# Self attention of a transformer's last stage: values as the weights, turned probabilities as the moving side, four heads side by side, the result copied out and turned back

## The reference, cut to what matters

```python
def _attention(src, Wq, bq, Wk, bk, Wv, bv, Wo, bo):      # 16 heads of 8 dims, 100 tokens
    q = (src @ Wq + bq).reshape(B, T, NHEAD, HEAD_DIM)
    k = (src @ Wk + bk).reshape(B, T, NHEAD, HEAD_DIM)
    v = (src @ Wv + bv).reshape(B, T, NHEAD, HEAD_DIM)
    scores = jnp.einsum('bqhd,bkhd->bhqk', q, k) * HEAD_DIM ** (-0.5)
    probs = jax.nn.softmax(scores, axis=-1)
    out = jnp.einsum('bhqk,bkhd->bqhd', probs, v).reshape(B, T, d)
    return out @ Wo + bo
```

## Time and profile before

| | us |
|---|---|
| median of three runs | 2578.37 (2575.73 to 2595.78) |
| the profiled execution, its time | 2595.61 |
| its span | 2593.8 |
| the self attention's 64 pieces in it | 1896.5 to 2348.6, 452.1 |
| the experts behind it | 2348.6 to 2593.8, 245.2 |

### The profile page before, as it was taken

The page is one execution under the profiler, slowest core; times in us unless marked ns, Lnnn a source line. Parts: engine busy times, 40 slices in busy tenths (PEclk is TensorE's granted clock), DMA queues, the critical chain, the costliest instruction groups (busy, mean ns, idle before and its releaser), DMA issues. The chain is left out here.

```text
span 2593.8 us, 44760 instructions
## 1 busy us (share of the span) xinstructions
PE 2236.1 (86%) x17786; PEld 1541.0 (59%) x17786; DVE 1608.6 (62%) x3886; ACT 1306.4 (50%) x2135; POOL 521.8 (20%) x428
## 2 busy tenths in 40 slices
PE   4689995565699999999999999999789999999997
PEld 3446663343355556555555556565557877777776
DVE  5734443777578787877878778888233444443433
ACT  3545553555156666666666666666523333333333
POOL 1400002332322122221222212222021111111111
PEclk8789995555599999999999999999865555558999
DMA  4036660000232223322333223332210010000000
GB/s 148 1 107 188 187 183 0 6 18 20 76 106 82 93 95 110 103 96 72 105 110 107 84 82 108 107 107 88 74 34 17 17 32 1 1 1 1 10 8 10
DMA packets 89100, 181.15 MB, mean 70 GB/s; under 512 B 5906, under 2 KB 63162, under 8 KB 88510
## 3 DMA queue, kind: packets, MB, share of 16 engines
q1 hardware_dynamic: 88894, 178.30, 20.9%
HBM read 95.24 MB, written 11.65 MB: 41 GB/s over the span
## 5 line engine op out<-in xcount | busy, mean ns | idle before, releaser
L1414 DVE TENSOR_REDUCE b_part_max<-psum 128x1 f32<-128x482 f32 (+3 forms) x1248 | 737.5, 650 | 187.2 <-PE psum L1291 173.3
L1204 ACT ACTIVATE b_PT<-psum 128x800 f32<-128x800 f32 x768 | 616.5, 836 | 386.6 <-PE psum L1310 380.4
L1291 PE MATMUL psum<-b_KH,b_QBD 64*128 64x482 f32 (+1 forms) x1152 | 421.5, 442 | 46.3 <-DVE b_part_max L1414 43.4
L1310 PE MATMUL psum<-b_QS,b_KS 64*128 64x200 f32 x3072 | 438.5, 288 | 0.5 <-ACT b_PT L1204 0.3
L1310 PEld LDWEIGHTS psum<-b_QS,b_KS 64*128 64x128 f32 x3072 | 339.6, 187 | 16.2 <-issue 12.1
L1326 PE MATMUL psum<-b_PT,b_V 128*32 128x200 f32 x6144 | 341.0, 339 | 0.6 <-ACT b_PT L1204 0.6
L1291 PEld LDWEIGHTS psum<-b_KH,b_QBD 64*128 64x128 f32 x1152 | 196.5, 188 | 198.0 <-DVE b_part_max L1414 118.5
L1326 PEld LDWEIGHTS psum<-b_PT,b_V 128*32 128x32 f32 x6144 | 159.8, 109 | 149.0 <-ACT b_PT L1204 82.3
L1127 POOL TENSOR_TENSOR b_KL<-b_KF,b_KH 128x1444 fp32r<-128x1444 f32 x32 | 106.8, 3337 | 691.5 <-PE psum L1310 669.4
L1651 ACT COPY c_PT<-psum 100x800 f32<-100x800 f32 x64 | 52.9, 826 | 297.7 <-PE psum L1801 297.7
L1812 PEld LDWEIGHTS psum<-c_VS,c_PT 100*100 100x100 f32 x1024 | 159.7, 257 | 33.1 <-ACT c_PT L1651 32.7
(11 more groups left out here) (269 smaller groups left out, 3586.8 us busy)
## 6 DMA issues: line engine op xcount, KB each, us to landing
b_KS<-b_KH SPq DMA_DIRECT2D x64, 722.0 KB
a_CT<-in_ctxt SPq DMA_DIRECT2D x32, 722.0 KB, 4.2
b_CT<-in_ctxt SPq DMA_DIRECT2D x32, 722.0 KB, 4.3
b_KS<-b_KL SPq DMA_DIRECT2D x32, 722.0 KB
a_CN<-in_ctxn SPq DMA_DIRECT2D x32, 704.0 KB
att_scratch<-b_AO SPq DMA_DIRECT2D x32, 200.0 KB, 1.9
c_AIN<-att_scratch SPq DMA_DIRECT2D x8, 800.0 KB
b_MB<-in_mask SPq DMA_DIRECT2D x32, 180.5 KB, 4.3
```

The costliest lines, as they stand in the source:

```text
L1204: nc.scalar.activation(PT[:, kt % 2, 2 * a:2 * a + 2, :], psum[:, 2 * a:2 * a + 2, 0:TG], ACT.Exp).then_inc(sem["pt_ready"], 1)
L1291: m = mm(bank(b, D, size), QBD[rows, j % 2, tile * D:(tile + 1) * D], KH[rows, j % 2, at_:at_ + size], start=True, stop=True)
L1310: m = mm(bank(p, D, 2 * T, (s % 2) * 2 * T), KS[rows, j % 2, s, kt * D:(kt + 1) * D], QS[rows, j % 2, s * 2 * T:(s + 1) * 2 * T], start=Tr ...
L1414: v.tensor_reduce(part_max[0:rows, q, c:c + 1], bank(b, rows, CHUNKS[c][1]), AX.X, ALU.max)\
```

## The change

In `weigh` the two sides change places: a head's values, 8 columns and 24 of ones, are the weights (100x32), and the turned probabilities (100 columns) move. Four heads lie side by side in the array's columns (`tile_position=(0, 32 * r)`) and write partitions 32r to 32r+31 of bank 6: dims of heads by tokens. ACT copies the bank to OS (`outputs`), PE turns it back with four transposes into bank 7 (`back`), and `divide` reads bank 7, where the sum now is the ninth of 32 columns of each head. As bank 7 is shared, `back` waits for the step before it to be read, and each step after it waits for `divide`. The gate's product stands behind `turn_pieces` now.

```diff
-        VS = sb("VS", [T, 2, GROUP, HEADS, HD + 1])
+        VS = sb("VS", [T, 2, GROUP, HEADS, 32])
+        OS = sb("OS", [D, TG])
...
-            pl.memset(VS[:, :, :, :, HD:HD + 1], 1.0).then_inc(sem["c_cleared"], 1)
+            pl.memset(VS[:, :, :, :, HD:], 1.0).then_inc(sem["c_cleared"], 1)
...
+            def outputs(m):
+                act.wait_ge(sem["fo_psum"], 2 * m + 2)
+                if m:
+                    act.wait_ge(sem["back_psum"], m)
+                nc.scalar.copy(OS[:, :], bank(6, D, TG)).then_inc(sem["os_ready"], 1)
...
+                if s % 2 == 0 and k:
+                    outputs(k // 2 - 1)
...
 weigh:
-                    pe.wait_ge(sem["fu_ready"], m)
+                    pe.wait_ge(sem["os_ready"], m)
                 for a in range(8):
-                    x_ = mm(bank(6, T, HD + 1, (8 * c + a) * (HD + 1)), PT[:, k % 2, a // 4, t.ts_(a % 4)],
-                            VS[:, u % 2, j, 8 * c + a, :], start=True, stop=True)
+                    r, q = a % 4, 2 * c + a // 4
+                    x_ = mm(psum[32 * r:32 * r + 32, 6, q * T:(q + 1) * T], VS[:, u % 2, j, 8 * c + a, :],
+                            PT[:, k % 2, a // 4, t.ts_(r)], start=True, stop=True, tile_position=(0, 32 * r), skip_group_check=True)
...
+            def back(m):
+                pe.wait_ge(sem["os_ready"], m + 1)
...
+                for q in range(4):
+                    x_ = nc.tensor.transpose(bank(7, T, D, q * D), OS[:, t.ts_(q)], ident)
+                x_.then_inc(sem["back_psum"], 1)
...
 PE's loop over the pieces:
+                if s % 2 == 0 and k:
+                    back(k // 2 - 1)
+                turn_pieces(k)
                 if s == 0 and b >= 2:
                     gate(b - 2)
-                turn_pieces(k)
...
 divide:
-                dve.wait_ge(sem["fo_psum"], 2 * m + 2)
+                dve.wait_ge(sem["back_psum"], m + 1)
-                fo = bank(6, T, width).rearrange("p (h d) -> p h d", h=HEADS)
+                fo = bank(7, T).rearrange("p (h d) -> p h d", h=HEADS)
```

More of the change, by code:

```diff
@@ L100 @@
 C_SIGNALS = """
[L101 to L104, removed]
+attx_psum b2_psum back_psum big_loaded c_chain c_cleared fe_ready fk_psum fk_ready fo_psum fpT_psum fpT_ready fq_psum
+fq_ready fs_psum fu_ready fv_psum fv_ready gate_psum gate_used gexp_ready gsub_ready hb_ready kbd_ready moe_h_psum
+moe_h_ready moe_y_psum moe_y_used os_ready out_ready out_scaled r_used sub_ready u_ready wT_psum wT_ready w_ready
+wo_psum x_ready xb_ready xin_ready y_ready y_scaled
 """.split()
@@ L1718, in _ @@
                     turned2(b - 1)
+            outputs(BATCH - 1)
             weights_turned(0)
@@ L1756, in attended @@
                     pe.wait_ge(sem["fv_ready"], u)
+                    pe.wait_ge(sem["fu_ready"], (u - 1) * GROUP)
                 if u >= 3:
@@ L1771, in keys @@
                 pe.wait_ge(tokT[0], u + 1)
+                if u:
+                    pe.wait_ge(sem["fu_ready"], (u - 1) * GROUP + 2)
                 mm(bank(7, D, TG), w("fk"), HT[:, :], start=True, stop=True).then_inc(sem["fk_psum"], 1)
@@ L1779, in values @@
                 pe.wait_ge(sem["fq_ready"], u + 1)
+                if u:
+                    pe.wait_ge(sem["fu_ready"], (u - 1) * GROUP + 3)
                 project(7, HT, w("fv"), sem["fv_psum"])
@@ L1809, in weigh @@
                 if m and not c:
-                    pe.wait_ge(sem["fu_ready"], m)
+                    pe.wait_ge(sem["os_ready"], m)
                 for a in range(8):
-                    x_ = mm(bank(6, T, HD + 1, (8 * c + a) * (HD + 1)), PT[:, k % 2, a // 4, t.ts_(a % 4)],
-                            VS[:, u % 2, j, 8 * c + a, :], start=True, stop=True)
+                    r, q = a % 4, 2 * c + a // 4
+                    x_ = mm(psum[32 * r:32 * r + 32, 6, q * T:(q + 1) * T], VS[:, u % 2, j, 8 * c + a, :],
+                            PT[:, k % 2, a // 4, t.ts_(r)], start=True, stop=True, tile_position=(0, 32 * r), skip_group_check=True)
                 x_.then_inc(sem["fo_psum"], 1)
+            def back(m):
+                u, j = divmod(m, GROUP)
+                pe.wait_ge(sem["os_ready"], m + 1)
+                if j == 0:
+                    if u:
+                        pe.wait_ge(tokT[1], u)
+                    else:
+                        pe.wait_ge(sem["x_ready"], 2)
+                if j == 1:
+                    if u < LAST:
+                        pe.wait_ge(tokT[0], u + 2)
+                    else:
+                        pe.wait_ge(sem["r_used"], u)
+                if j == 2:
+                    pe.wait_ge(sem["fq_ready"], min(u + 2, UNITS))
+                if j == 3:
+                    if u:
+                        pe.wait_ge(tokT[2], u)
+                    else:
+                        pe.wait_ge(sem["fv_ready"], 2)
+                for q in range(4):
+                    x_ = nc.tensor.transpose(bank(7, T, D, q * D), OS[:, t.ts_(q)], ident)
+                x_.then_inc(sem["back_psum"], 1)
             def turn1(u):
@@ L1827, in outer @@
                 pe.wait_ge(tokT[1], u + 1)
+                pe.wait_ge(sem["fu_ready"], min((u + 1) * GROUP + 1, BATCH))
                 project(7, OT, w("fo"), sem["wo_psum"])
@@ L1841, in gate @@
                 pe.wait_ge(tokT[2], u + 1)
+                pe.wait_ge(sem["fu_ready"], min((u + 2) * GROUP, BATCH))
                 project(7, YT[:, u], t.W[:, WGATE:WGATE + EXPERTS], sem["gate_psum"], EXPERTS)
@@ L1918, in _ @@
             pe.wait_ge(sem["big_loaded"], 32)
+            back(BATCH - 1)
             gate(LAST - 1)
@@ L1988, in divide @@
                 u, j = divmod(m, GROUP)
-                dve.wait_ge(sem["fo_psum"], 2 * m + 2)
+                dve.wait_ge(sem["back_psum"], m + 1)
                 if u >= 2:
                     dve.wait_ge(turned[1], u - 1)
-                width = HEADS * (HD + 1)
-                fo = bank(6, T, width).rearrange("p (h d) -> p h d", h=HEADS)
+                fo = bank(7, T).rearrange("p (h d) -> p h d", h=HEADS)
                 link(v.reciprocal(inv[:, m % 2, :], fo[:, :, HD]))
```

## The result

The changed kernel takes 2447.11 us in the median of four runs (2444.84 to 2449.78) against 2577.89 before (four runs, 2575.73 to 2595.78). The ratio over all these runs is 0.9474, 95% interval [0.9435, 0.9513]; that of the two medians is 0.949. On another chip, beside the experiments, it was 2451.4 against 2583.6, 0.9475 [0.9429, 0.952]. The kernel before spreads more than this pair says: on the three chips of the experiments its medians of seven runs are 2595.2, 2583.6 and 2594.3, its runs 2569 to 2601. The forecast was 2459, range 2398 to 2524. The profiled execution of after has a span of 2443.1 us, 150.7 less than that of before.

A forecast was written before the change was run, and what follows sets the result against it. PE at 1.2 GHz was taken to bound the 64 pieces. A unit of 57.8 us becomes 43.0, midway between cold 49.8 and warm 36.1; eight save 119, so 2578.4 - 119 = 2459 us, range 2398 to 2524.

The forecast's parts named there:

- The bound: Stage c's 64 pieces, 452.1 us: PE sets the time, busy in 435 of them, at 1.2 GHz.
- The new `weigh`: The 16 passes of `weigh`: 1.34 to 0.48 us at full clock, 2.52 to 0.90 at the lower; 11.4 saved per unit.
- Back and copy: ACT's copy of bank 6 costs 0.48 us; PE's four transposes 0.45 at full clock, 0.86 at the lower.
- the ring: Warm loop from `back` through divide, subtract, exponent, pieces, keep, exponent and copy to `back`: 7.4 us per two slots.
- The warm unit: One unit of the pieces at full clock: 36.1 us, saving 21.7, or 174 over eight units.
- half of 5.62: Warm price of `attended` in a unit: half its 5.62 us less what it covers, put at 2.7.
- The share of the two clocks: Clock full for part of each unit: midway between 49.8 and 36.1 us, so 43.0, saving 119 over eight.
- The base: Saving of 119 us taken from the median 2578.4, though the profiled execution took 2595.6, 17 above it.
- Clock low as before: Rival for the pieces: the clock stays low, saving 64 us, program 2514; chance 27%.
- Full throughout: Rival for the pieces: clock full nearly throughout, saving 174 less 6 for a cold first unit, program 2410; chance 26%.
- Ring binds cold: Rival: ACT or VectorE queues eat PE's gain of 64 us even at the low clock, program 2565 to 2590; chance 4%.
- Tiles one after another: Rival: `weigh`'s four tiles do not run side by side, a cold one takes 3.0 us, program 2636; chance 4%.

The follow-up runs named there:

- The wide kernel: Kernel before with 100 moving columns instead of 9 in each product of `weigh`, old layout kept: 2438.52 us, ratio 0.9392.
- the changed kernel's second profile: The changed kernel run again without edits, on another chip beside three edits of it: 2451.36 us.
- fillers: Three unused products of 112 columns ahead of `weigh` in each odd slot: 2451.66 us in the changed kernel, 2396.44 without copy and `back`.
- the second profile: The kernel before, unchanged, profiled once more: 2577.46 us, span 2575.7.
- both edits of the ring together: Changed kernel with `subtract` of the next piece ahead of `divide`, and three unused products ahead of `weigh` in odd slots: 2410.78 us, ratio 0.9326.
- tiles in pairs: Changed kernel with `weigh`'s heads in the order 0, 4, 1, 5, 2, 6, 3, 7: 2452.30 us, ratio 0.9454.
- no turning back: Changed kernel without the copy to OS and the four transposes, attention's result left out: 2420.99 us, ratio 0.9316.
- subtract first: Changed kernel with VectorE's `subtract` of the next piece ahead of `divide` and `gate_first` in even slots, plus three PE waits: 2418.64 us, ratio 0.9353.

## Why the prediction held, step by step

**The bound.** Right: PE at the lower clock. The wide kernel leaves PE all its passes, changes the clock, and takes 6% off the program, so most hung on the clock.

**The new `weigh`.** 0.48 at the full level, as forecast from stage b's row. The cold price, forecast at 0.90, can be read only where the clock falls in a unit; on the chain of the changed kernel's second profile:

```profile
1994.73 0.83 PE psum L1828 x16
1995.56 1.58 PE psum L1807 x4
1997.14 1.04 PE psum L1853 x4
```

The scores behind it take 1.58; at the lower level they took 1.59 in the earlier trace rows.

**Back and copy.** 0.50 for the copy on the chain, forecast at 0.48; `back` takes PE 0.48 up to its next operation, forecast at 0.45, but `divide` waits for its last pass, so the ring pays 0.66 where 0.50 was put down. At the lower level it is 1.04 on the chain, forecast at 0.86 for PE. The drain that the Trainium skill ("TensorEngine Tiling (Array Packing)", Key Properties) names for a change of tiling mode can't be told apart here, since the 0.48 holds it; no run here shows it. The larger fill of VS took 2.66 us and stayed ahead of an input that came 3.3 us later, so it cost nothing, as forecast.

**The warm unit.** 36.1 forecast, 35.7 measured. This was the best of the steps, and the ring the right picture: one `back` ends 8.0 us after the other with `enter` between them (1949.59 to 1957.58), and the bare ring was put at 7.4. Three terms were off, and partly cancel. POOL's spread for slot 6 was missing: 9.1 us from `back` to `back` there, 0.75 of it idle PE. The four copies of bank 7 were put at 2.2; ACT's next operation starts 0.37 to 0.48 after each, 1.7 in all. And half of 5.62 is not the price of a warm `attended`, since the clock rose in the midst of that row: it takes 3.71, and more of it is covered by ACT and VectorE than was thought. Taking `divide` out of the ring gave 33 us, taking copy and `back` out 55 with the clock held by fillers on both sides.

**The share of the two clocks.** Wrong in size, and the weakest step: half and half was the middle between two cases, not worked out from a row. I took 43.0 us for a unit; it is 36 to 39. The clock is 0.89 over the pieces and 0.95 from 1928 to 2163, which is six units, so it was at the lower level for about a tenth of these and not for half. By this step the profiled execution should have lost 119 us and lost 149. The mechanism was much as described: full from `attended` on and lost behind a thin place, in four of six times in slot 6 behind `middle` and the wait for POOL's spread (the units at 0.95 and 0.91 take 37.3 - 35.7 = 1.6 and 38.9 - 35.7 = 3.2 us longer), won back in the dense ones; it is lost more seldom and won back faster than I had it. In each of those four slots PE waits 1.10 us for `keep` and 0.75 for the spread; the unit at 1.00 has the same two waits and keeps the clock, so the waits by themselves do not settle it.

**The base.** This one hid the other. The 149 belong to an execution of before that was itself 17 us above the median, 18 above the second profile, because of its clock, and I took the saving from the median without asking where those 17 us were. Against the medians the gain is 131, so the total came out 12 us from the forecast with two errors of 30 and 18 that partly cancel. That closeness is luck; the direction, the ring and the prices are not.

**Rivals.** Clock low as before (2514): no. Full throughout (2410): near it in most units, 35.7 to 38.9 us where it had 36.1, but 37 us above it in the program; that both edits of the ring together come to 2410.8 is a meeting of numbers by another way. Ring binds cold: the clock rose, so no unit shows it. Tiles one after another (2636): no, 1.18 against 0.48 shows that they run together. Its price was worked out at the lower clock and no run has tested it there; at a clock of 0.96 the 0.7 us more per `weigh` cost 8 to 12 us in all.

**Cause of the gain.** The change makes PE's passes fewer and shorter, and that alone does not account for the gain; the clock does. With the old layout and a held clock the time is 2438.5 (2433.9 to 2440.4); on that chip the changed layout with tiles in pairs, whose `weigh` is 0.50, has 2452.3. What the swap saves on PE at full clock, 0.9 us per `weigh`, ends in waiting: PE idles 6.5 us of a unit, the ring sets its length. In the old layout at the same clock PE sets it: its five lines hold 88.5% of the chain over the 40 us shown. What the shorter passes would have brought at the old clock, forecast at 64 us, no run shows, since none has the new layout and the old clock.

What stays open: why the clock is lost so seldom in the changed kernel, with PE idle for 6.5 us of each unit, and how a tile of 32 columns counts against one of 128. No run here tells these apart.

## What to carry to other kernels

Before pricing an edit to TensorE's work, read the granted clock of the stretch: if it is the lower one, ask first which thin stretch loses it, and try to fill that with moving columns where the weights bound the pass anyway and they cost little (0.07 us for sixteen passes here). Work moved off the critical engine only pays up to the next ring, so walk that ring; here an exchange of two VectorE steps in it was worth another quarter of what the change brought (33 us to 132). And take a saving from the execution whose rows it was made from, or find out why that one differs from the median.

## What the runs showed of the hardware that was not expected

Ninety-one useless columns per pass cost 0.07 us in a `weigh` of 1.34 at the full clock, brought the clock from 0.56 to 1.00, and with it 6% of the program; what they would cost at the lower clock no run shows. Three small products per odd slot, pure extra work for PE, made two kernels faster (no turning back: 2421.0 to 2396.4; subtract first: 2418.6 to 2410.8), though not the changed kernel itself (2451.4 and 2451.7). Dense work of 1.3 to 2.9 us ahead of each thin stretch did not carry the clock over all of them, whether it was transposes (0.68) or products (0.66). Passes on the four tiles need not come in the order 0, 1, 2, 3 to run together: with two heads in a row on a tile a `weigh` still took 0.50, with four in a row 1.18.
